# A node table of 98 places a lane instead of 105, and 109 rows of edges instead of 110, in a two-layer graph network

## The chip, the core and the metric

The kernel runs on one core of a Trainium2 chip. The metric is the device time of one execution in microseconds (us). All data are float32 or int32.

## What is computed

12,500 nodes with 256 features, 212,500 edges sorted by destination (12,500 of them are self edges). After a layer norm and a batch norm, two GIN layers follow: each sums the features of every node's neighbours, adds the node itself, and applies two dense layers with a batch norm between them.

```python
N, E, D = 12500, 212500, 256
h = relu(layernorm(x))
h = batchnorm(h, g0, b0)
for W1, b1, g, bt, W2, b2 in layers:          # two
    agg = segment_sum(h[src], dst, N)         # E rows of 256, sorted by dst
    h = relu(batchnorm((h + agg) @ W1 + b1, g, bt))
    h = relu(h @ W2 + b2)
out = x + relu(h)
```

## The kernel before

**Nodes.** Node n lies in lane n % 128 (the SBUF partition) and block n // 128; there are NB = 98 blocks. The sums and the features stand in `acc`, one column stretch of DP = 260 words (1040 bytes) for each block. For the gathers the features are also written to a table in HBM. In it a node has the place `lane * PITCH + block`, with PITCH = 105: 98 places with a node and 7 empty ones (zeros) in each lane, NPOS = 13,440 in all.

**Copies of the table.** Sources in one row of edges are sorted by place, and one gathered element may cover two edges whose places are 1, 2, 3, ... apart. For larger steps the table is stored four more times: the copy of stride s (3, 4, 5, 7) has places q, q + s, q + 2s, ... next to each other (`place_in`: residue q % s times NPOS / s, plus q // s). So NPOS must be a multiple of 3, 4, 5 and 7. A copy is written from `acc` with DMAs on SP's queue, generated by `strided_places`: for one stride it takes the lanes in `stride // gcd(stride, PITCH)` sets, and for each set and each residue of the blocks one DMA, of that many lanes by n blocks. `copies_of_blocks` does so for a group of GROUP = 14 blocks; GROUPS = 7 groups make the table. The empty places get zeros by `spare_places`, once for both tables, at L560.

**Edges.** The edges are cut into NR = 110 rows of LR = 1932 (the last is shorter), one row to a lane of the lists, sorted on VectorE within 2048 slots. The first RAWS = 14 rows are gathered edge by edge from the natural table in layer 0 while the sort still runs ("raw", 224 gathers of 128 rows at L679). For the others each row becomes T = 8 tiles of 128 elements; a tile is one indirect DMA on POOL (L697) of 128 elements with 4, 3, 3, 2, 2, 2, 2, 1 table rows each (`ROWS_OF`). Tiles 0 to 5 read the strided copies or the table, tiles 6 and 7 the natural table alone. PE multiplies each tile by one-hot matrices from VectorE (L830, 17 products a row) and VectorE adds the sums to `acc` (L1582).

**Order.** Layer 0: SP loads x and the edges, writes the empty places (L560), stores the table (L565), then issues the copies (L600), each behind a wait for the progress of the raw tiles (`raw_done`), so that they lie beside them. POOL's first strided gather waits for all copies (`copies_stored`, L711), and so does ACT's scaling of the sums (L1101). Then comes walk 0 over rows 14 to 109. After the batch norm the second product (`second_product`, `dense`) writes the new features block by block. SP stores them to the second table, chunk by chunk of 7 blocks (L565, last pieces L576); from the second chunk on it issues copies after each store, until 8 x 128 table rows are issued (`BESIDE`, L613); the rest follows after the last store (L617). POOL gathers tiles 6 and 7 of the first TWICE = 80 rows as soon as the natural table stands, and then waits for the copies of all groups (`group_stored`, L709) before the strided tiles of rows 0 to 79 and all tiles of the rest. ACT scales the sums of a group once its copies have landed (L1104).

If a check on the lists fails (a row that doesn't fit its tiles), `is_general` selects a slow general path on all engines.

Of the kernel before, what the change touches and what calls it, by code (L numbers as in the profile page):

```python
# [14 lines left out]
P = 128  # L15
# [7 lines left out]
NB = (N + P - 1) // P  # L23
# [7 lines left out]
DP = 260  # L31

PITCH = NB + 7
NPOS = P * PITCH
STRIDES = (3, 4, 5, 7)
TABLE = (1 + len(STRIDES)) * NPOS + 8

LR = 1932
NR = (E + LR - 1) // LR
TAIL = E - (NR - 1) * LR
SORT = 2048
# [37 lines left out]

UP = 512
PAD_SRC = 1000 * P + P - 1
SRC_CAP = 14000
REMOVED = float(2 ** 22)
DROPPED = float(2 ** 126)
WHOLE = 1.5 * 2 ** 23  # L90
# [7 lines left out]
RAWS = 14  # L98
# [6 lines left out]
RAW_HOTS = 3  # L105
LAST_EDGES = LR - (RAW - 1) * P
RAW_LISTS_AT = 8
# [5 lines left out]

NODES_PER_ROW = LR * N / E
NODE_TOL = 60
# [91 lines left out]

assert TWICE % 2 == 0 and NB % (2 * CH) == 0 and TAIL < LR and NR < P and RAW % AT_ONCE == 0
assert all(max(b for b in TILE_BEFORE[:k + 1] if b is not None) >= k - LANDINGS for k in range(LANDINGS, len(TILES)))
# [3 lines left out]
assert all(min(RAWS, PAIR_END[q] + 1) <= raws_merged_by(PAIR_ENDS[0][q]) for q in range(NPAIR))  # L213
assert all(2 * KC * P * (q % 2 + 1) <= raws_merged_by(PAIR_ENDS[0][q]) * DP for q in range(2))
assert PAIRS_BESIDE * RAW_GROUPS >= NPAIR and RAW % RAW_GROUP == 0 and 0 < LAST_EDGES <= P and 4 * SORT + RAW_INSIDE * DP <= RING * DP
assert SRC_CAP > NPOS + UP and all(NPOS % s == 0 and i + 1 == min(s, 6) - 2 for i, s in enumerate(STRIDES))
assert NB * (QUARTER + 1) <= RING * DP and 4 * SORT <= RING * DP and X_SLOTS * CH * D <= RING * DP

F32 = mybir.dt.float32
# [6 lines left out]
def build(nc, x, src, dst, g0, b0, W1a, b1a, g1, bt1, W1b, b1b, W2a, b2a, g2, bt2, W2b, b2b, out):  # L226
# [4 lines left out]
    with ctx:  # L231
        def sb(name, shape, dt=F32):
            return ctx.enter_context(nc.sbuf_tensor(name, shape, dt))
# [11 lines left out]
        src_rows = rows[:, GIVEN:2 * GIVEN]  # L245
        node_steps = rows[:, 2 * GIVEN:2 * GIVEN + LR]
        self_edges = rows[:, 3 * GIVEN:3 * GIVEN + LR]
# [30 lines left out]
        early = sb("early", [P, max(RAWS * DP, 4 * KC * P + 3 * KC * D + 2 * D)])  # L278
# [178 lines left out]
        def tile_rows(k, first, width):  # L457
            at_row = (TILE_AT[k] + first) * DP
            return rows[:, at_row:at_row + width]
# [17 lines left out]
            return bank[:, :].rearrange("p (j g) -> p j g", g=P)[:, :, 0:NR]  # L477

        def places(table, b0, b1):
            return table[0:NPOS, :].rearrange("(p b) f -> p b f", b=PITCH)[:, b0:b1, :]  # L480

        def block_rows(b0, b1, step=1):
            return acc[:, :].rearrange("p (b f) -> p b f", f=DP)[:, b0:b1:step, :]
# [1 line left out]
        def place_in(stride, q):  # L485

            return (1 + STRIDES.index(stride)) * NPOS + q % stride * (NPOS // stride) + q // stride

        def places_of(table, first_row, steps):
            return bass.AP(table.tensor, table.offset + first_row * DP, [[step * DP, n] for step, n in steps] + [[1, DP]])  # L490

        def strided_places(table, stride, b0, b1, of):

            lanes = stride // math.gcd(stride, PITCH)
            for lane in range(lanes):
                for first in range(b0, min(b0 + stride, b1)):
                    n = len(range(first, b1, stride))
                    yield (places_of(table, place_in(stride, lane * PITCH + first),
                                     [(lanes * PITCH // stride, P // lanes), (1, n)]),
                           of(first, n, stride)[lane:P:lanes])  # L500

        def copies_of_blocks(table, b0, b1):
            for stride in STRIDES:
                yield from strided_places(table, stride, b0, b1, lambda first, n, step: block_rows(first, first + (n - 1) * step + 1, step))

        zeros = early[:, 0:RAWS * DP].rearrange("p (b f) -> p b f", f=DP)

        def spare_places(table):
            yield places(table, NB, PITCH), zeros[:, 0:PITCH - NB]
            for stride in STRIDES:  # L510
                yield from strided_places(table, stride, NB, PITCH, lambda first, n, step: zeros[:, 0:n])
            yield table[TABLE - 8:TABLE, :], zeros[0:8, 0]

        EDGE_PIECES = ((0, 96), (96, NR - 1 - 96), (NR - 1, 1))
        EDGE_DMAS = 2 * len(EDGE_PIECES)
        CONST_DMAS = 1 + 8
        LATE_DMAS = 5
        SPARE = 16 * sum(1 for _ in spare_places(tables[0]))
        GROUP_COPIES = 16 * sum(1 for _ in copies_of_blocks(tables[0], 0, GROUP))
        COPIES = GROUPS * GROUP_COPIES  # L520
# [17 lines left out]
        def _(sp):  # L538
# [19 lines left out]
            for table in tables:  # L558
                for to, of in spare_places(table):
                    sp.dma_start(to, of).then_inc(spare_stored, 16)  # L560

            def store_rows(t, c, done, count):
                sp.wait_ge(done, count)
                b0, b1 = c * CH, (c + 1) * CH
                sp.dma_start(places(tables[t], b0, b1), block_rows(b0, b1)).then_inc(table_stored, 16)  # L565
# [6 lines left out]
            def store_last_rows():  # L572
                for at_block, end in LAST_PIECES:
                    b0, b1 = (NCH - 1) * CH + at_block, (NCH - 1) * CH + end
                    sp.wait_ge(y_out, b1)
                    sp.dma_start(places(tables[1], b0, b1), block_rows(b0, b1)).then_inc(table_stored, 16)  # L576
# [61 lines left out]
        def _(pool):  # L638
# [35 lines left out]
            for g in range(RAWS):  # L674
                for j in range(RAW):
                    k = g * RAW + j
                    if k >= RAW_SLOTS:
                        pool.wait_ge(raw_done, k - RAW_SLOTS + 1)
                    pool.indirect_dma_start(  # L679
                        raw_rows[k % RAW_SLOTS], None, tables[0][0:NPOS, :],  # L680
                        bass.IndirectOffsetOnAxis(raw_src[:, j * RAWS + g:j * RAWS + g + 1], 0)
# [6 lines left out]
            def gather(layer, g, t):  # L688
# [5 lines left out]
                if before is not None and before + 1 > freed:  # L694
                    freed = before + 1
                    pool.wait_ge(tiles_done, freed)
                pool.indirect_dma_start(  # L697
                    tile_rows(k, 0, ROWS_OF[t] * DP), None, tables[layer][0:NPOS if t >= LAST_STRIDED else TABLE, :],
                    bass.IndirectOffsetOnAxis(src_all[:, g * T + t:g * T + t + 1], 0)
# [426 lines left out]
        def _(dve):  # L1126
# [148 lines left out]
            def step(ins):  # L1275
                nonlocal sorted_to
                ins.then_inc(sort_step, 1)
                sorted_to += 1

            def after():  # L1280
                dve.wait_ge(sort_step, sorted_to)
# [76 lines left out]
            dve.wait_ge(steps_squared, 1)  # L1358
            step(dve.tensor_scalar(third_ints, keys, float(UP * P), float(SRC_CAP * P), ALU.add, ALU.min))
            after()  # L1360
# [44 lines left out]
            step(dve.tensor_scalar(key_ints, a, float(SINGLE), None, ALU.add))  # L1405
            step(dve.scalar_tensor_tensor(second, other_ints, float(SRC_CAP), second, ALU.is_ge, ALU.max))
            after()
# [393 lines left out]
```

## Time and profile before

| | |
|---|---|
| median of 3 runs | 2776.4 us (2771.52 to 2776.82) |
| profiled execution | 2784.43 us, its span 2782.6 us |
| PE matmul busy | 2371.1 us, 85% |
| PE weight load busy | 1827.6 us, 66% |
| POOL busy | 1815.2 us, 65% |
| DVE busy | 1739.1 us, 62% |
| ACT busy | 551.3 us, 20% |
| granted clock, mean | 0.94 |

The profile in 40 slices of 70 us; a digit is the busy share in tenths:

```profile
POOL 2058777777777777777740477677777777777720
PEclk8687766999999999999989899999999999999999
DMA  9387998888888888888848999888888888888868
GB/s 309 141 261 224 285 306 254 250 260 251 253 253 255 254 255 254 254 254 254 254 153 279 328 334 325 285 283 286 287 284 284 287 285 282 260 254 253 253 203 270
```

The first slices hold the loads, the layer norm and the store of the first table; slices 3 to 7 the raw tiles with the copies of layer 0; 7 to 20 walk 0; 21 to 22 the second product; 22 to 25 the copies of layer 1 with the natural gathers; 25 to 38 the strided gathers of walk 1. Engines: PE matmul, PEld its weight load, DVE VectorE, ACT ScalarE, POOL GpSimd, SP the engine whose queue issues the plain DMAs; SPq is time in which that queue is busy issuing.

### The profile page before, as it was taken

To read this page: it belongs to the slowest core of one execution; us is meant where nothing else is said; L and a number is where in the kernel's file an instruction comes from. 1 tells how busy PE (TensorE), PEld (TensorE's weight loads), DVE (VectorE), ACT (ScalarE), POOL (GpSimd) and SP (SyncE) were. 2 spreads that over 40 slices of the span, in tenths; PEclk is the share of its full clock that TensorE was granted. 3 is DMA by queue.
4 is the path that set the end of the run, shared out by engine and by line. 5 is a ranking of instruction groups with operands and counts; after the bars stand their busy time and mean duration, and the time that the engine had idled before them with its cause. 6 is when DMAs were issued, how large, how long until landed. Compare 5 with 4: busy or idle time off the path is not lost.

```text
span 2782.6 us, 30723 instructions
## 1 busy us (share of the span) xinstructions
PE 2371.1 (85%) x10215; PEld 1827.6 (66%) x10215; DVE 1739.1 (62%) x3502; ACT 551.3 (20%) x1605; POOL 1815.2 (65%) x1894
## 2 busy tenths in 40 slices
PE   1466777999999999999979566699999999988979
PEld 1134433878877777777758444588888888776767
DVE  7999997755555555555548577555555555544459
ACT  8975544300000000000009311000000000000038
POOL 2058777777777777777740477677777777777720
PEclk8687766999999999999989899999999999999999
DMA  9387998888888888888848999888888888888868
GB/s 309 141 261 224 285 306 254 250 260 251 253 253 255 254 255 254 254 254 254 254 153 279 328 334 325 285 283 286 287 284 284 287 285 282 260 254 253 253 203 270
DMA packets 309364, 734.28 MB, mean 264 GB/s; under 512 B 41510, under 2 KB 183730, under 8 KB 309198
## 3 DMA queue, kind: packets, MB, share of 16 engines
q0 software_dynamic: 149184, 550.97, 63.2%
q1 hardware_dynamic: 160014, 181.25, 20.8%
q8 instruction: 86, 1.41, 0.2%
q14 instruction: 80, 0.66, 0.1%
HBM read 579.47 MB, written 152.59 MB: 263 GB/s over the span
## 4 chain that ended last, share of the span: by engine, by line
PE 51%; DMA 23%; POOL 8%; SPq 8%; ACT 5%; issue 4%; DVE 1%; DVEq 0%; ACTq 0%; POOLq 0%
PE agg_ps L830 35%; DMA rows<-node_rows,src_all 17%; SPq L617 7%; PE sort_ps L955 6%; PE sort_ps L872 5%; POOL rows L697 5%; DMA rows<-node_rows,raw_list 4%; PE sort_ps L876 2%; DMA raw_more<-node_rows,raw_list 2%; PE agg_ps L779 2%; ACT acc L1001 2%; POOL raw_more L679 2%; ACT lane_code L988 1%; ACT lane_code L977 1%; POOL rows L679 1%
## 5 line engine op out<-in xcount | busy, mean ns | idle before, releaser
L697 POOL DMA_INDIRECT rows<-node_rows,src_all x1648 | 1558.2, 946 | 642.6 <-issue 346.4
L830 PE MATMUL agg_ps<-rows,work 128*128 128x256 f32 (+1 forms) x7004 | 1630.3, 387 | 188.9 <-DMA rows<-node_rows,src_all 140.8
L830 PEld LDWEIGHTS agg_ps<-rows,work 128*128 128x128 f32 x7004 | 1297.7, 191 | 494.3 <-issue 133.9
L1582 DVE SCALAR_TENSOR_TENSOR acc<-agg_ps,in_first,acc 128x256 f32 (+1 forms) x286 | 138.7, 485 | 944.1 <-PE agg_ps L830 856.7
L1032 ACT ACTIVATE bn_root<-bn_var 128x2 f32<-128x2 f32 x3 | 0.6, 203 | 1860.2 <-DVE bn_var L1168 1860.2
L679 POOL DMA_INDIRECT rows<-node_rows,raw_list x124 | 129.2, 1042 | 174.8 <-DMA node_rows<-acc 137.3
L1534 DVE TENSOR_TENSOR work<-lane_code,lane_ps 128x1024 f32<-128x1024 f32 (+1 forms) x206 | 228.1, 1107 | 1.0 <-issue 1.0
L955 PE MATMUL sort_ps<-early,work 128*128 128x256 f32 x784 | 175.3, 388 | 22.1 <-ACT work L1117 11.5
L955 PEld LDWEIGHTS sort_ps<-early,work 128*128 128x128 f32 x784 | 140.2, 194 | 57.5 <-issue 25.6
L1543 DVE TENSOR_TENSOR work<-lane_code,lane_ps 128x640 f32<-128x640 f32 x206 | 167.7, 814 | 0.0
L1117 ACT ACTIVATE work<-acc,bn_shift,bn_scale 128x128 f32<-128x128 f32 x392 | 166.5, 485 | 3.3 <-DVE bn_shift L1179 2.8
L779 PE MATMUL agg_ps<-rows,lane_code 128*128 128x257 f32 (+1 forms) x248 | 109.8, 562 | 59.6 <-DMA rows<-node_rows,raw_list 56.6
L1582 DVE SCALAR_TENSOR_TENSOR acc<-agg_ps,in_second,acc 128x256 f32 (+1 forms) x286 | 136.1, 476 | 0.0
L1524 DVE SCALAR_TENSOR_TENSOR work<-lane_ps,lane_code,work 128x128 f32<-128x128 f32 x412 | 130.5, 342 | 0.0
L679 POOL DMA_INDIRECT raw_more<-node_rows,raw_list x100 | 110.6, 1106 | 30.5 <-issue 23.5
L779 PEld LDWEIGHTS agg_ps<-rows,lane_code 128*128 128x128 f32 (+1 forms) x248 | 55.2, 260 | 106.6 <-DMA rows<-node_rows,raw_list 79.3
L1106 ACT ACTIVATE acc<-acc,self_scale 128x257 f32<-128x257 f32 (+1 forms) x196 | 79.0, 495 | 193.4 <-DMA node_rows<-acc 176.8
L1538 DVE TENSOR_TENSOR work<-lane_code,lane_ps 128x384 f32<-128x384 f32 x206 | 112.7, 547 | 0.0
L1345 DVE TENSOR_TENSOR work<-work,sort_ps 128x512 f32<-128x512 f32 x168 | 108.0, 684 | 2.9
L779 PE MATMUL agg_ps<-raw_more,lane_code 128*128 128x257 f32 x200 | 81.3, 530 | 32.2 <-DMA raw_more<-node_rows,raw_list 31.9
L872 PE MATMUL sort_ps<-early,w_a 128*128 128x256 f32 x392 | 107.2, 396 | 1.3 <-DVE early L1611 1.3
L1345 DVE TENSOR_TENSOR sort_ps<-work,sort_ps 128x512 f32<-128x512 f32 x168 | 108.2, 690 | 0.0
(246 smaller groups left out, 1844.8 us busy)
## 6 DMA issues: line engine op xcount, KB each, us to landing
node_rows<-acc SPq DMA_DIRECT2D x113, 260.0 KB, 6.3
rows<-node_rows,src_all POOLq DMA_INDIRECT x1648, 4.4
node_rows<-acc SPq DMA_DIRECT2D x27, 910.0 KB, 4.3
node_rows<-acc SPq DMA_DIRECT2D x57, 390.0 KB, 5.4
node_rows<-acc SPq DMA_DIRECT2D x28, 650.0 KB, 8.6
node_rows<-acc SPq DMA_DIRECT2D x114, 130.0 KB, 4.6
acc<-in_x SPq DMA_DIRECT2D x13, 896.0 KB, 11.0
rows<-in_x SPq DMA_DIRECT2D x13, 896.0 KB, 7.3
```

The lines of the kernel that those rows point to most:

```text
L617: sp.dma_start(to, of).then_inc(group_stored[i], 16)
L679: pool.indirect_dma_start(raw_rows[k % RAW_SLOTS], None, tables[0][0:NPOS, :], bass.IndirectOffsetOnAxis(raw_src[:, j * RAWS + g:j * RAWS ...
L697: pool.indirect_dma_start(tile_rows(k, 0, ROWS_OF[t] * DP), None, tables[layer][0:NPOS if t >= LAST_STRIDED else TABLE, :], bass.IndirectO ...
L779: pe.matmul(bank[:, 0:D + 1], raw_hots[n % RAW_HOTS][0:edges, (j - first) * P:(j - first + 1) * P], raw_rows[k % RAW_SLOTS][0:edges, 0:D + ...
L830: mm = pe.matmul(bank[:, 0:width], hot[:, unit * P:(unit + 1) * P], tile_rows(k, row, width), start=(start and n == 0), stop=(stop and n = ...
L872: mm = pe.matmul(to, w_a[layer][:, k, o * P:(o + 1) * P], sum_major[:, m % 2, k, :], start=(o == 0 and k == 0), stop=(last and k == KC - 1 ...
L955: mm = pe.matmul(mm_ps[b % 2][:, 0:D], act_major[:, b % CH, k, :], w_b[layer][:, k, :], start=(k == 0), stop=(k == KC - 1))
L1117: ins = act.activation(act_major[:, b % CH, k, :], half_block(b, k), ACT.Relu, bias=bn_shift[:, k:k + 1], scale=bn_scale[:, k:k + 1])
L1345: step(dve.tensor_tensor(place, low, high, op))
L1534: dve.tensor_tensor(hot[:, 0:2 * n * P].rearrange("p (j f) -> p j f", f=2 * P), codes[:, 0:n].unsqueeze(2).to_broadcast([P, n, 2 * P]), la ...
L1543: dve.tensor_tensor(hot[:, FIRST_AT[0] * P:(FIRST_AT[0] + m) * P].rearrange("p (j f) -> p j f", f=P), lanes[:, 0:m].unsqueeze(2).to_broadc ...
L1582: dve.scalar_tensor_tensor(to, sums, lanes[:, g:g + 1], to, ALU.mult, ALU.add).then_inc(sums_added, 1)
```

## The change

PITCH becomes 98, so that the 128 lanes fill the first 12,544 places (PLACES) without gaps. NPOS becomes 12,600, the next multiple of 3, 4, 5 and 7; the 56 spare places follow the whole table. A row of edges has 1950 instead of 1932, which makes 109 rows instead of 110. `strided_places` now counts the lanes of each set, since 128 isn't a multiple of the new numbers of sets. The spare places are written as one stretch for each copy and residue.

```diff
-PITCH = NB + 7
-NPOS = P * PITCH
+PITCH = NB
+PLACES = P * PITCH
+NPOS = 12600
...
-LR = 1932
+LR = 1950
...
-SRC_CAP = 14000
+SRC_CAP = 13500
...
-assert SRC_CAP > NPOS + UP and all(NPOS % s == 0 and i + 1 == min(s, 6) - 2 for i, s in enumerate(STRIDES))
+assert PAD_SRC // P + (P - 1) * PITCH + UP >= SRC_CAP > NPOS + UP and NPOS > PLACES and all(NPOS % s == 0 and i + 1 == min(s, 6) - 2 for i, s in enumerate(STRIDES))
...
-            return table[0:NPOS, :].rearrange("(p b) f -> p b f", b=PITCH)[:, b0:b1, :]
+            return table[0:PLACES, :].rearrange("(p b) f -> p b f", b=PITCH)[:, b0:b1, :]
...
-                                     [(lanes * PITCH // stride, P // lanes), (1, n)]),
+                                     [(lanes * PITCH // stride, len(range(lane, P, lanes))), (1, n)]),
                            of(first, n, stride)[lane:P:lanes])
...
-        zeros = early[:, 0:RAWS * DP].rearrange("p (b f) -> p b f", f=DP)
+        zeros = early[:, 0:DP]
 
         def spare_places(table):
-            yield places(table, NB, PITCH), zeros[:, 0:PITCH - NB]
+            yield table[PLACES:NPOS, :], zeros[0:NPOS - PLACES]
             for stride in STRIDES:
-                yield from strided_places(table, stride, NB, PITCH, lambda first, n, step: zeros[:, 0:n])
-            yield table[TABLE - 8:TABLE, :], zeros[0:8, 0]
+                for first in range(PLACES, PLACES + stride):
+                    n = len(range(first, NPOS, stride))
+                    yield table[place_in(stride, first):place_in(stride, first) + n, :], zeros[0:n]
+            yield table[TABLE - 8:TABLE, :], zeros[0:8]
```

## Rows read from the trace of the kernel before

**Rows 1.** The page: the span, and the chain that ended last.

```profile
span 2782.6 us, 30723 instructions
...
PE 51%; DMA 23%; POOL 8%; SPq 8%; ACT 5%; issue 4%; DVE 1%; DVEq 0%; ACTq 0%; POOLq 0%
```

**Rows 2.** POOL's timeline: start, duration, engine, line, tile, count, idle time before and its releaser.

```profile
469.07 0.94 POOL L697 DMA_INDIRECT rows<-node_rows,src_all  x1 [0.30 <-issue]
...
1430.84 0.95 POOL L697 DMA_INDIRECT rows<-node_rows,src_all  x1 [0.30 <-issue]
1558.84 0.94 POOL L697 DMA_INDIRECT rows<-node_rows,src_all  x1 [127.06 <-DMA node_rows<-acc]
...
1770.30 0.94 POOL L697 DMA_INDIRECT rows<-node_rows,src_all  x1 [11.69 <-DMA node_rows<-acc]
...
2668.69 0.94 POOL L697 DMA_INDIRECT rows<-node_rows,src_all  x1 [0.30 <-issue]
```

**Rows 3.** Busy time and instructions of each engine in stretches of 100 us.

```profile
core 0: us, PE busy (x) PEld busy (x) DVE busy (x) ACT busy (x) POOL busy (x), PEclk, DMA share, GB/s
700.00:800.00 100.00, 98.68 (x447) 79.48 (x446) 55.15 (x120) 0.00 (x0) 75.63 (x81) 1.00 0.82 254
2500.00:2600.00 100.00, 90.28 (x396) 71.10 (x396) 49.37 (x104) 0.00 (x0) 75.63 (x81) 1.00 0.82 254
```

**Rows 4.** Timeline of SP's queue, merged by line.

```profile
41.27 39.49 SPq L560 DMA_DIRECT2D node_rows<-early  x66
110.99 45.22 SPq L565 DMA_DIRECT2D node_rows<-acc  x14
...
161.85 290.53 SPq L600 DMA_DIRECT2D node_rows<-acc  x217
...
1475.80 1.53 SPq L613 DMA_DIRECT2D node_rows<-acc  x2
...
1552.39 210.42 SPq L617 DMA_DIRECT2D node_rows<-acc  x156
```

**Rows 5.** The chain of 1430 to 1790: shares by line, three pieces of it.

```profile
by line: SPq L617 56.1%; PE sort_ps L955 23.2%; issue 5.6%; PE agg_ps L830 5.5%; DMA node_rows<-acc 2.3%; PE sort_ps L872 1.5%; DMA rows<-node_rows,src_all 1.3%; SPq L613 1.2%; PE sort_ps L876 1.0%; SPq L576 0.9%; POOL rows L697 0.3%; DVE e
...
1597.29 6.87 SPq L617
...
1695.26 0.61 SPq L617
...
1761.12 8.32 DMA node_rows<-acc
```

**Rows 6.** DMA view of 1475 to 1770: packets, and each queue's share of 16 engines.

```profile
q1 hardware_dynamic: 55952, 64.31, 70.9%
q0 software_dynamic: 10240, 31.96, 32.7%
```

**Rows 7.** DMA view of 9 to 16.9, of 2779.8 to 2781.15, of 2781.2 to 2782.6.

```profile
DMA packets 840, 1.88 MB, mean 238 GB/s; under 512 B 60, under 2 KB 679, under 8 KB 840
...
GB/s 303 364 364 364 334 303 455 273 334 364 394 303 303 455 303 273 394 394 273 304 274 91 183 182 304 364 303 334 394 394 303 303 425 243 182 61 61 0 0 0
DMA packets 403, 0.38 MB, mean 282 GB/s; under 512 B 32, under 2 KB 403, under 8 KB 403
...
q1 hardware_dynamic: 403, 0.38, 82.8%
...
DMA packets 98, 0.09 MB, mean 61 GB/s; under 512 B 14, under 2 KB 98, under 8 KB 98
```

**Rows 8.** DMA issues of the whole span: KB each, us from issue to landing.

```profile
node_rows<-acc SPq DMA_DIRECT2D x113, 260.0 KB, 6.3
...
work<-in_dst SPq DMA_DIRECT2D x1, 98.2 KB
...
out<-acc SPq DMA_DIRECT2D x1, 84.0 KB
```

**Rows 9.** DMA view of 170 to 450: the gathers' queue.

```profile
q0 software_dynamic: 9813, 27.22, 36.2%
```

## The prediction

> **What bounds the kernel now.** I read the page's chain first. It names PE for half the span, which makes the walks look like matrix work, but a chain follows only the last releaser; POOL and SP stand in it too [rows 1]. So I read POOL's timeline. In both walks a gather starts every 1.25 us, whatever PE does: 768 strided gathers of layer 0 from 469.07 to 1430.84, 160 natural ones of layer 1 from 1558.84 on, which end 11.69 us before 1770.30, and 720 strided ones from there to 2668.69: (1430.84 - 469.07) / 767 and (2668.69 - 1770.30) / 719 are both 1.25 [rows 2]. The stretches of 100 us say the same: 81 gathers and 75.63 us of POOL in each, PE busy 99% in one and 90% in the other [rows 3]. The walks run at POOL's issue rate.
>
> Between the walks stands a second bound. A strided gather reads one of four strided copies of the table, and the first one waits until all copies have landed. SP issues them: 217 DMAs from 161.85 in layer 0, and in layer 1 61 between the table stores from 1475.80 on and 156 more until 1761 [rows 4]. In layer 1 the last copy lands at 1761.12 + 8.32 = 1769.4 and the gather follows at 1770.30; the chain of that stretch gives SP's L617 56.1% [rows 5]. In layer 0 it doesn't bind: the last copy is issued at 452.4, and the gather at 469.07 follows its predecessor after the usual 0.30 us [rows 2, 4]. What the copies cost is DMA time: from 1475 to 1770 the 16 engines are busy 70.9 + 32.7 = 103.6% [rows 6].
>
> **The change, part by part.**
>
> *One row of edges less.* 109 rows instead of 110: each walk loses a full row of 8 tiles at 1.25 us, 10 us. The last 8 strided gathers of each walk are what falls away, and the walks are POOL's from their first gather to their last, so **-20 us** counts in full. 1950 columns instead of 1932 in some setup operations on VectorE, and 30 edges instead of 12 in the last raw tile of a row, cost nothing I can measure: those are below 1% of operations that are not the longest there.
>
> *Spare places.* 66 stores of zeros become 42 smaller ones. They run from 41.27 to 80.8, and SP then waits for ACT's rows until 111 [rows 4]: 30 us of cover. If that were gone, 24 issues of 0.6 us would be worth 14 us. I take 0.
>
> *The copies.* With a pitch of 98 the lanes fall apart into classes: a stride s needs s/gcd(s, pitch) sets of lanes, each with its own DMAs. Before, that was 1, 4, 1, 1 sets for strides 3, 4, 5, 7; now it is 3, 2, 5, 1. For 14 blocks that makes 9 + 8 + 25 + 7 = 49 DMAs instead of 3 + 16 + 5 + 7 = 31; 343 a layer instead of 217. The 7168 rows of 1040 bytes for each group of 14 blocks stay. What changes is how many lanes a DMA has: 128 and 32 before; now 43, 43, 42 for stride 3; 64 for stride 4; 26, 26, 26, 25, 25 for stride 5; 128 for stride 7.
>
> Which engines such a DMA uses is the question. The DMA view counts a packet for each row and, below 512 bytes, one for each engine that ends its share. Around 2780 us two stores of 128-row blocks end with 32 such packets, 16 each. The last store has 84 rows (84 KB): 98 packets, 84 rows and **14** endings, so 14 engines with 6 rows each, not 16. The six loads of edges have 96, 13 and 1 rows, each twice; they end with 60 = 2 x (16 + 13 + 1) packets [rows 7, 8]. Two readings fit all four sizes. *Equal shares*: the engines used are the largest number up to 16 that divides the rows. *Rounded shares*: each engine takes ceil(rows/16), and the last may take fewer. They part at 43: equal shares give **1** engine (43 is prime), rounded shares 15. The 84 rows exclude a third reading, rows dealt out one by one, which would have used 16 engines. Between the other two the trace doesn't decide. I take equal shares, since every DMA in it has the same number of rows on each engine that it uses, and no row shows an engine with an odd rest.
>
> The Trainium skill ("DMA: Bandwidth & Descriptors", section "Why a DMA increments its semaphore by 16 and not by 1") states equal shares, too: the largest count up to 16 that divides the slowest dimension of both sides, and on the queues of SP always the lowest-numbered engines. By it 43 lanes run on one engine, and it speaks against this change; by rounded shares the sum would be the 2774 us below. The trace agrees at 84, 13 and 1; no run here shows 43.
>
> Load of the busiest engine for each group, in rows of 1040 bytes: stride 3: two sets of 43 lanes x 14 blocks on one engine, 1204, and 42/14 x 14 = 42; stride 4: 2 x 4 x 14 = 112; stride 5: 3 x 2 x 14 = 84 on 13 engines and 2 x 5 x 14 = 140 on 5; stride 7: 8 x 14 = 112. If the shares always begin at the same engine, it carries 1694 rows against 448 before; in 7 groups 11,858 against 3136. If each DMA began elsewhere, the order in SP's queue would still put up to six 43-lane DMAs behind each other, but they could overlap; that is the low side.
>
> Price of a row on one engine: two looks. Near the end 0.38 MB take 82.8% of 16 x 1.35 us, so 21.2 GB/s of a busy engine, 49 ns for 1040 bytes; from 1475 to 1770, with all engines full, 64.31 MB take 70.9% of 16 x 295 us, 19.2 GB/s, 54 ns. The best slices show 364 GB/s, 45.7 ns [rows 6, 7]. With 15 engines nearly idle the first is nearer: 49 ns x 11,858 = **581 us** a layer.
>
> *Layer 0.* The copies begin at 161.85. The same engine carries a sixteenth of the 224 raw gathers, 8 rows each: 1.86 MB at 20.7 GB/s (rate of the gather queue: 31.96 MB in 32.7% of 16 x 295 us [rows 6]), 90 us. End of the copies 161.85 + 581 + 90 = 833. The raw tiles and VectorE's sort still end near 468 beside it. The first strided gather moves from 469 to 833: **+364 us**; all behind it moves along. Behind the copies in SP's queue stand the weight loads (L602 on), which wait for a point inside the walk anyway; ACT's scaling of the sums waits for the copies too (L1101), as it did, and takes 6 us for the blocks that the first row needs.
>
> *Layer 1.* From 1475.80 (all times as if nothing had moved before): copies 581, the 12 chunks of table stores still to come (910 KB each, a sixteenth, 21.2 GB/s) 33, natural gathers 31.96 MB / 16 at 20.7 GB/s, 97. End 2187 against 1769.4: **+417 us**. The second product's 80 us, the 160 natural gathers (200 us at 1.25) and the wait for table stores queued behind 43-lane copies (SP gets to the last of them after about 3300 rows on that engine, 160 us) all end before: 1475.8 + 160 + 33 + 200 = 1869. ACT's scaling of the sums waits group by group for the same copies (L1104), VectorE's adds wait for ACT, and so the natural visits up to row 79, which reach block 73, wait for the sixth of seven groups; that lands a seventh of the time, 100 us, before the last. After the copies the walk goes at 1.25 us a gather again.
>
> Sum against the profiled execution, 2784.4 us (span 2782.6 [rows 1]): + 364 + 417 - 20 = 3545. The median of the runs lies 8 us lower: **3537 us**.
>
> **Rivals.**
>
> *Rounded shares.* 43 lanes on 15 engines at 3 rows. The busiest engine carries 42 x 3 + 112 + 140 + 112 = 490 rows a group, 42 more than before, 294 in a layer, 14 us at 49 ns. In layer 0 the copies end near 459 (452.4 and 6.3 us to landing [rows 8]), so 14 us later is 4 us of wait; in layer 1 all 14 count. 2784.4 + 4 + 14 - 20 - 8 = **2774**: not slower. It decides if a 43-row DMA ends on more than about ten engines. For it: the trace has no prime above 16. Against it: see above. Small shifts make it a little faster or the same.
>
> *SP's issue as the bound.* If the rows are spread, 126 more issues a layer remain, at 0.61 us each [rows 5], 77 us, if SP can't queue ahead. Layer 1 alone exposes it: 2784.4 + 77 - 20 - 8 = **2833**. Against it: 343 x 0.61 = 209 us is less than the 294 us that the data takes in layer 1, and SP's issues there stretch to 6.87 us when the engines are full, so it does queue ahead.
>
> *A cheaper or dearer engine.* At 45.7 ns a row (gathers at that rate too) layer 0 is +317 and layer 1 +367: 3440. At 54 ns and raw gathers at 16.8 GB/s (27.22 MB in 36.2% of 16 x 280 us [rows 9]) it is +444 and +487: 3687. Same mechanism, other size. A lone queue that can't keep its engine full would go further; nothing here prices that, so the top gets 100 us more.
>
> *It doesn't do what it says.* 1950 edges in 2048 slots leave denser rows; should one row not fit its tiles, the kernel takes its general path, with loops of 98 steps for every four columns, many times slower. Nothing in the profile speaks for it; 0.02.
>
> **How the numbers follow.** Equal shares on one engine 0.87, rounded shares 0.08, SP's issue 0.03, general path 0.02. The range holds eight in ten within the first case: from 3440, less 50 for overlap between DMAs, to 3687 plus 100: **3390 to 3787**. It leaves out the two middle cases and the general path. A measurement of this kernel tells about 0.2% apart, 6 us. Faster by that takes rounded shares with less than their full price, 0.04; within it 0.05; slower 0.91.
>
> **What would show it.** POOL's wait for the copies near 833 us instead of none, and again some 417 us longer in layer 1; DMA share of slices falling to one or two tenths with GB/s under 50 while 43-lane copies run; SP's issues of L600 and L617 taking many us each in groups of six; gathers 8 fewer in each walk, still at 1.25 us. The prediction is wrong if the DMA share stays at nine tenths during the copies; then it is the rounded case. It is off in size if the slices show another rate for the one engine than 21 GB/s.

## The result, and the profile after

The changed kernel takes 3574.53 us (median of 4 runs, 3571.87 to 3575.25), the one before 2775.11 us (4 runs, 2771.52 to 2776.82). The ratio is 1.288, 95% interval 1.286 to 1.2901: slower by 799 us, as forecast. 3537 us was predicted, 1% less than measured and inside the range. Of all runs told here one, of e8, was far from the others of its kernel (3991.24 us, at a mean granted clock of 0.567 instead of 0.94); the ratios leave it out.

The page of the changed kernel: span, POOL's busy tenths, DMA share and rate in 40 slices of 89 us, and the engines' shares of the chain.

```profile
span 3572.6 us, 30769 instructions
...
POOL 1187720003777777777710074310177777777750
...
DMA  5455532226888888888824466432488888888877
GB/s 169 171 150 160 155 111 83 84 83 189 264 251 253 254 254 252 253 253 253 253 81 144 145 183 178 143 109 84 144 284 284 285 284 284 284 273 253 253 227 246
...
PE 38%; SPq 28%; DMA 16%; POOL 9%; issue 5%; ACT 4%; DVE 0%; DVEq 0%; POOLq 0%; ACTq 0%
```

The PE share of the chain fell from 51 to 38%, SP's queue rose from 8 to 28% [rows 1]. Slices 7 to 9 and 22 to 28 (from 1) are new. In 7 to 9 POOL stands still and the rate is 83 or 84 GB/s; 22 to 28 hold the copies of layer 1, with the natural gathers in 24 to 27, and end at 84 GB/s. The walks between and behind have the rates of before. The mean granted clock was 0.837 instead of 0.94, but the table below shows the walks no longer than before, so the clock is not what costs the time.

POOL's timeline gives the stages (start, duration, line, idle time before and its releaser): the last raw gather, the first strided gather of layer 0, its last, the first strided gather of layer 1, its last.

```profile
470.30 0.94 POOL L682 DMA_INDIRECT rows<-node_rows,raw_list  x1 [0.30 <-issue]
...
850.25 0.94 POOL L700 DMA_INDIRECT rows<-node_rows,src_all  x1 [379.00 <-DMA node_rows<-acc]
...
1802.01 0.95 POOL L700 DMA_INDIRECT rows<-node_rows,src_all  x1 [0.30 <-issue]
...
2567.62 0.94 POOL L700 DMA_INDIRECT rows<-node_rows,src_all  x1 [167.19 <-DMA node_rows<-acc]
...
3456.88 0.95 POOL L700 DMA_INDIRECT rows<-node_rows,src_all  x1 [0.30 <-issue]
```

SP's queue, merged by line, shows what POOL waited for: the stores of zeros and of the first table, the copies of layer 0 (L603), the first of layer 1 (L616) and the rest (L620).

```profile
41.52 16.42 SPq L563 DMA_DIRECT2D node_rows<-early  x42
...
111.21 45.20 SPq L568 DMA_DIRECT2D node_rows<-acc  x14
...
162.35 682.91 SPq L603 DMA_DIRECT2D node_rows<-acc  x343
...
1846.29 39.07 SPq L616 DMA_DIRECT2D node_rows<-acc  x5
...
2047.27 515.39 SPq L620 DMA_DIRECT2D node_rows<-acc  x249
```

Against [rows 2, 4]:

| stage | before | after | difference |
|---|---|---|---|
| first strided gather of layer 0 | 469.07 | 850.25 | +381.2 |
| walk 0, first to last gather | 961.8 | 951.8 | -10.0 |
| last gather of walk 0 to the first copy of layer 1 | 45.0 | 44.3 | -0.7 |
| first copy of layer 1 to the first strided gather | 294.5 | 721.3 | +426.8 |
| walk 1, first to last strided gather | 898.4 | 889.3 | -9.1 |
| rest | 113.9 | 115.7 | +1.8 |
| span | 2782.6 | 3572.6 | +790.0 |

The table adds up. Two waits for copies are +808 us, and the row less gives 19 us back. The mechanism can be looked at directly. An *ending* is, as in the prediction, one of the packets below 512 bytes, which each engine leaves when its share of a DMA ends. The DMA view of 580 to 617, where the moving data is of 43-lane copies alone and POOL is idle:

```profile
GB/s 11 24 22 21 20 21 21 21 20 21 21 20 21 21 21 20 21 21 20 21 21 21 20 21 21 20 21 21 20 21 21 21 20 21 21 20 21 21 21 20
DMA packets 746, 0.77 MB, mean 21 GB/s; under 512 B 3, under 2 KB 746, under 8 KB 746
...
q1 hardware_dynamic: 746, 0.77, 6.7%
```

21 GB/s through the whole stretch, and 6.7% of 16 engines, which is 107% of a single one. Of the 746 packets only 3 are endings: three 43-lane DMAs end here, one ending each. The chain of 520 to 620 shows SP held up by them (start, duration): a copy of 43 lanes and 5 blocks is 215 rows, and the next issue waits 10.58 us for it, 49.2 ns a row; with 4 blocks 8.69 us. A copy of 26 lanes (stride 5) takes SP 0.81 us.

```profile
by line: SPq L603 109.1%; issue 2.2%
...
524.38 10.58 SPq L603
...
535.01 8.69 SPq L603
...
552.04 0.81 SPq L603
```

Do copies of one queue simply run one after another, each on whatever engine? The end of a run of 43-lane copies tells. Three windows of the DMA view, 530.5 to 540.8, 541 to 544, and 541.1 to 548.5:

```profile
DMA packets 208, 0.22 MB, mean 21 GB/s; under 512 B 0, under 2 KB 208, under 8 KB 208
...
DMA packets 61, 0.06 MB, mean 21 GB/s; under 512 B 0, under 2 KB 61, under 8 KB 61
...
GB/s 22 22 17 22 22 17 22 22 22 17 22 22 22 17 22 22 22 112 264 225 253 253 113 236 191 230 264 219 231 253 253 315 337 354 343 337 360 332 337 343
DMA packets 1220, 1.21 MB, mean 163 GB/s; under 512 B 61, under 2 KB 1220, under 8 KB 1220
```

A copy of 5 blocks ends between the first two windows; the last one of this run (43 lanes, 4 blocks, 172 rows) follows it and at 49 ns a row needs until about 549.5. Yet from 544.3 on the copies issued behind it (42 lanes, from 543.74) move on the other engines, and 61 endings come before it can have ended. So copies don't wait for each other as such. What waits is a row on an engine that is still busy with earlier ones, and 43-lane copies that follow each other do wait: they are on the same engine.

The count of endings of the whole run is the sharpest reading. The page's line of packets:

```profile
DMA packets 303335, 720.47 MB, mean 202 GB/s; under 512 B 41132, under 2 KB 181096, under 8 KB 303170
```

By equal shares the packets below 512 bytes must be: 1856 gathers x 16 = 29,696; 2048 elements of 4 bytes in 8 loads of vectors; the endings of the 98 loads and stores that aren't copies or zeros, 1524; zeros 402; and for each group of 14 blocks 6 x 1 + 3 x 14 + 8 x 16 + 15 x 13 + 10 x 5 + 7 x 16 = 533, times 14 groups, 7462. The sum is 41,132, which is the page's number to the packet. With 43 lanes on 15 engines it would be 1176 more from that stride alone.

### The profile page after: what moved, and what is told of

It is laid out like the page before. It is cut to its first block, busy times and chain, and to the rows that moved or that the text cites. A ratio compares the mean times of both kernels' runs of the same rounds, so it can differ in the third digit from the quotient of the medians.

```text
span 3572.6 us, 30769 instructions
## 1 busy us (share of the span) xinstructions
PE 2382.7 (67%) x10147; PEld 1818.0 (51%) x10147; DVE 1730.5 (48%) x3486; ACT 552.7 (15%) x1605; POOL 1803.9 (50%) x1878
## 2 busy tenths in 40 slices
DMA packets 303335, 720.47 MB, mean 202 GB/s; under 512 B 41132, under 2 KB 181096, under 8 KB 303170
## 4 chain that ended last, share of the span: by engine, by line
PE 38%; SPq 28%; DMA 16%; POOL 9%; issue 5%; ACT 4%; DVE 0%; DVEq 0%; POOLq 0%; ACTq 0%
PE agg_ps L833 25%; SPq L620 14%; DMA rows<-node_rows,src_all 12%; SPq L603 10%; POOL rows L700 6%; PE sort_ps L958 5%; PE sort_ps L875 4%; SPq L616 3%; DMA rows<-node_rows,raw_list 2%; PE sort_ps L879 2%; POOL rows L682 1%; POOL raw_more L682 1%; DMA raw_more<-node_rows,raw_list 1%; ACT acc L1004 1%; PE agg_ps L782 1%
## 5 line engine op out<-in xcount | busy, mean ns | idle before, releaser
L782 PE MATMUL agg_ps<-raw_more,lane_code 128*128 128x257 f32 x200 | 92.7, 567 | 35.9 <-DMA raw_more<-node_rows,raw_list 34.8
```

Source lines behind the costliest of these rows:

```text
L782: pe.matmul(bank[:, 0:D + 1], raw_hots[n % RAW_HOTS][0:edges, (j - first) * P:(j - first + 1) * P], raw_rows[k % RAW_SLOTS][0:edges, 0:D + ...
```

## The experiments

The experiments are called by the first part of their labels (e5 and so on) and told in the order of the argument. Each is compared with runs of the kernel before that were made beside it; their medians were 2777.26 us (e3 to e6), 2773.37 (e1, e7 to e9), 2774.13 (e10) and 2778.21 (e12 to e14).

**Only the number of lanes (e5, e6).** The kernel before keeps its pitch of 105 and its 110 rows; only the stride-3 copies are cut, into neighbouring lanes.

```diff
-                    yield (places_of(table, place_in(stride, lane * PITCH + first),
-                                     [(lanes * PITCH // stride, P // lanes), (1, n)]),
-                           of(first, n, stride)[lane:P:lanes])
+                    at = 0
+                    for m in (43, 43, 42) if stride == 3 else (P // lanes,):
+                        l0 = lane + at * lanes
+                        yield (places_of(table, place_in(stride, l0 * PITCH + first),
+                                         [(lanes * PITCH // stride, m), (1, n)]),
+                               of(first, n, stride)[l0:l0 + (m - 1) * lanes + 1:lanes])
+                        at += m
```

> The kernel before (pitch 105, 110 rows), with one edit: each stride-3 copy of 128 neighbouring lanes is cut into 43, 43 and 42 neighbouring lanes. Same bytes, same places, 42 more DMAs a layer, no lane is skipped. Equal shares from the same first engine: two sets of 43 lanes x 14 blocks on one engine, so 1204 + 42 + 3 x 112 = 1582 rows a group on it, 11,074 a layer; at 50 ns a row, with the gathers' share, the copies of layer 0 end near 805 us (+336) and those of layer 1 take 683 instead of 294 us (+389): 3501 us. Rounded shares: 2776 to 2790 us. If what is slow were lanes with a step of 3 or 5 (the pattern in SBUF) or the change's new places in HBM, this kernel stays at 2776 us. If each additional DMA cost what it seems to in the changed kernel, (3574 - 2775 + 20) / 252 = 3.2 us: 84 more are 2776 + 273 = 3050 us.

Measured: 3462.27 us (one run), 39 us below the forecast. Rates of the DMA view from 700 to 780, and the end of POOL's wait in layer 0:

```profile
GB/s 321 266 26 21 21 21 21 21 21 21 122 21 21 21 21 21 21 21 21 21 21 122 21 21 21 21 21 21 21 24 218 183 177 192 196 244 342 341 313 306
...
784.58 0.94 POOL L701 DMA_INDIRECT rows<-node_rows,src_all  x1 [313.45 <-DMA node_rows<-acc]
```

The same 21 GB/s, in a kernel whose table, places, rows and lane steps are those of before. The wait in layer 0 is 313 us (the first strided gather at 784.58, forecast 805), and layer 1 takes 653.7 us (forecast 683), 47.8 ns for each of 13,666 rows; the rows were priced a little too high. The cut alone costs 685 us, so a loss of this size needs neither the step of the lanes nor the new places nor the denser rows. The packets of its page:

```profile
DMA packets 309364, 734.28 MB, mean 212 GB/s; under 512 B 41510, under 2 KB 183730, under 8 KB 309198
```

This is the line of the kernel before, number for number: 43, 43 and 42 lanes leave 1 + 1 + 14 endings, 128 lanes left 16.

> The same cut of the kernel before with other sizes: 48, 48 and 32 neighbouring lanes for stride 3. As many DMAs as with 43, 43 and 42, and the same bytes, but each size is a multiple of 16. Equal shares: 3 + 3 + 2 = 8 rows an engine and block, as with 128 lanes, so 2776 us, within 0.3%. A cost of each additional DMA: 3050 us by the price of 3.2 us, or by the 0.61 us of an issue 2776 + 26 = 2802 us at most.

The edit is the same with (48, 48, 32). Measured: 2786.23 us, ratio 1.0032 (1.0019 to 1.0044). As many DMAs as with 43, 43, 42, the same bytes, and 676 us less. It is 9 us above the kernel before, a little more than expected; more on that below.

```profile
DMA packets 310900, 734.29 MB, mean 264 GB/s; under 512 B 43046, under 2 KB 185266, under 8 KB 310734
```

43,046 against 41,510 endings: 1536 more. That is 3 residues x 14 groups = 42 triples of DMAs, and 6 more in the stores of zeros, 48, of 16 + 16 + 16 against 1 + 1 + 14 = 16 endings: 48 x 32 = 1536, exact.

**Numbers that divide, but badly (e14).** The same edit with (65, 63).

> The kernel before with stride 3 cut into 65 and 63 neighbouring lanes; neither is prime. Equal shares: 65 on 13 engines with 5 rows, 63 on 9 with 7, so 12 rows a block on the first engine instead of 8; 56 rows a group, 392 a layer, at 50 ns +20 us in layer 1 and up to +5 in layer 0: 2800 us. Rounded shares: 5 + 4 = 9 rows, +5 us: 2780 us. If every count that isn't a multiple of 16 went on one engine, 128 rows a block: above 3500 us.

Measured: 2799.44 us, ratio 1.008 (1.0065 to 1.0096); its page:

```profile
DMA packets 309652, 734.29 MB, mean 262 GB/s; under 512 B 41798, under 2 KB 184018, under 8 KB 309486
```

Equal shares give 13 + 9 endings for each pair of these DMAs and a total of 41,798 (rounded shares: 13 + 16, 42,134). The count is exact again, so equal shares hold for counts that aren't prime. The time agrees with the forecast, but less well than it looks: by POOL's timeline layer 1 took 303.7 us and layer 0 began 3 us later, +9 and +3 against before, where +20 and +5 were expected; the rest lies in the offset that is told below. On the fullest engine are 3528 rows of copies, 672 of stores and 1920 of gathers in layer 1: 303.7 us / 6120 = 49.6 ns, against 294.5 / 5728 = 51.4 before. With all engines equally full the row came out a little dearer.

**Mending the change, one count at a time (e3, e4).** In the changed kernel the same loop takes its pieces from a table; lanes that are neighbours within a set of step `lanes` stay so.

```diff
+                    for m in {43: [42, 1]}.get(len(range(lane, P, lanes)), [len(range(lane, P, lanes))]):
```

> The changed kernel, where each copy DMA of 43 lanes is split into 42 lanes and 1 lane; the 25- and 26-lane DMAs stay. 42 DMAs more a layer (385). Equal shares: 42 lanes go on 14 engines, 3 rows each, the single lane adds one; the first engine carries 2 x 14 x 4 + 42 + 112 + 224 + 112 = 602 rows a group instead of 1694. With gathers and stores 6918 rows in layer 1, 345 us at 50 ns against 294 before: +50; layer 0 ends near 465 to 470: 0 to +5; the row less -20: 2776 + 50 + 3 - 20 = 2809 us, 765 us faster than the changed kernel by adding DMAs. If the step of the lanes or the number of DMAs were the cause: 3574 us or more.

Measured: 2858.29 us (one run). 716 us of the loss go with 84 *more* DMAs in the two layers, so the number of DMAs was not their cause. The kernel is 49 us slower than expected: the strided gathers begin at 498 instead of 469 in layer 0, and layer 1 takes 362 us. This run doesn't say why; e4 and e7 point at the issues. Its page counts 42,616 endings, 1484 more than the change. The expectation, one ending for the single lane, would give 1176; with 5 + 5 + 4 endings for its copies of 5, 5 and 4 blocks it is 1484, exact. When only one lane is left, the blocks are the outermost dimension above one, and they are what is shared out.

```diff
+                    for m in {43: [32, 11], 25: [16, 9]}.get(len(range(lane, P, lanes)), [len(range(lane, P, lanes))]):
```

> The changed kernel with every bad count split: 43 lanes into 32 + 11, 25 into 16 + 9; 26 and 42 stay (13 and 14 engines). 65 DMAs a group, 455 a layer against 343 and 217. Equal shares: 3 x 42 + 112 + 140 + 112 = 490 rows a group on the fullest engine, as in the rounded case: layer 1 has 6134 rows, 307 us, +12; layer 0 hidden; 2776 + 12 - 20 = 2768 us. Issue as the bound: 455 x 0.61 = 278 us of issues in layer 1 beside 307 us of data; if they don't overlap fully, up to 60 us more, 2830 us. If the number of DMAs were the cause of the 800 us: above 4000 us.

Measured: 2923.76 us, ratio 1.0527 (1.0509 to 1.0544). Better shares, and slower by 65 us than e3. SP's queue in layer 0; from the chain two neighbouring issues of 32 and 11 lanes (stride 3) and two of 16 and 9 (stride 5); and the rates from 470 to 530:

```profile
162.33 367.16 SPq L607 DMA_DIRECT2D node_rows<-acc  x455
...
486.92 0.60 SPq L607
...
487.56 0.81 SPq L607
...
513.55 0.60 SPq L607
...
514.20 0.76 SPq L607
...
GB/s 135 64 52 52 49 343 328 277 275 265 157 149 149 119 170 242 347 317 268 216 194 137 69 106 90 94 82 90 60 58 57 42 46 52 52 52 41 200 345 297
```

455 issues in 367.16 us are 0.81 us each, waits included. The first pair moves 160 and 55 rows, 224 KB, and the rate there is about 149 GB/s; the second moves 16 x 3 rows, 50 KB, in 0.60 us and 9 x 3 rows, 28 KB, in 0.76 us, and the rate is 41 to 60 GB/s. In both stretches the rate is what the issues bring, so here the issue is the bound. An issue took 0.60 us with 16 or 32 lanes, 0.76 with 9, and 0.79 to 0.81 with 11, 26 or 42; in the changed kernel one of 25 lanes, on 5 engines, took 0.70 to 0.72. My expectation compared sums (278 us of issues, 307 us of data); it should have compared them stretch by stretch, since the rate follows the issues within a few us.

**Fewer, larger copies (e7, e8).** On e4, and for e8 on the kernel before. The first list is layer 1's, the second layer 0's.

```diff
-GROUPS = NB // GROUP
+BOUNDS = (0, 14, 42, 70, 98)
+GROUPS = len(BOUNDS) - 1
...
+        BOUNDS_0 = (0, 98)
...
-                    for to, of in copies_of_blocks(tables[1], i * GROUP, (i + 1) * GROUP):
+                    for to, of in copies_of_blocks(tables[1], BOUNDS[i], BOUNDS[i + 1]):
```

> The changed kernel with 43 lanes split into 32 + 11 and 25 into 16 + 9 as in e4, and with fewer, larger copies: layer 0 copies the whole table as one group of 98 blocks (65 DMAs instead of 455), layer 1 in four groups of 14, 28, 28 and 28 blocks (260 instead of 455). The share of the fullest engine is the same as in e4 (35 rows a block); only the number of issues falls. If e4 lost its 150 us because SP couldn't issue fast enough (its traces show 0.60 us for 16 or 32 lanes and 0.77 to 0.80 for 9, 11, 26 or 42), this one hides the issues: 260 x 0.7 = 182 us beside 307 us of data in layer 1, so 2776 + 12 - 20 = 2768 us, at most 2800 where the small stride-5 copies still starve the engines. If e4 lost them to the uneven shares or to small packets on some engines, it stays near 2924 us.

Measured: 2809.88 us, ratio 1.0132 (1.0116 to 1.0149). SP's queue in layer 0 and after the second product, and the end of POOL's wait in layer 1:

```profile
162.10 303.17 SPq L609 DMA_DIRECT2D node_rows<-acc  x65
...
1577.33 218.90 SPq L626 DMA_DIRECT2D node_rows<-acc  x172
...
1803.74 0.94 POOL L706 DMA_INDIRECT rows<-node_rows,src_all  x1 [21.59 <-DMA node_rows<-acc]
```

114 us better than e4 with the same shares, so most of e4's loss was the issues. It is still 10 us above the top of what was expected (2768 to 2800): layer 0 ends 13 us late, of which the single group of 98 blocks accounts for 8 (e8), and layer 1 takes 327 us instead of 294.5, of which the fuller engine was to cost 12. A further variant, with groups of 28, 28, 21 and 21 blocks in both layers (e11), has no result: in it `acc` could be overwritten before a copy had read it. So what is left of e7's loss isn't taken apart.

> The kernel before (pitch 105, 110 rows) with the groups of e7: 31 copies for the whole table in layer 0, 124 in layer 1. Its copies are limited by the engines' data in layer 1 (103.6% busy) and hidden in layer 0, so fewer issues are worth nothing: 2776 us, within 0.3%. If the groups themselves were worth something, it shows here and has to be taken off e7.

Measured: 2786.2 us (median of four runs, 2784.45 to 2787.25), ratio 1.0046 (1.003 to 1.0062), just outside what was expected: layer 0 begins its walk 8 us later, layer 1 takes 285.5 us, 9 less. The groups by themselves gain nothing.

**The parts alone (e9, e1).** e7 and the changed kernel with 110 rows.

```diff
-LR = 1950
+LR = 1932
```

> e7 with 1932 edges a row, so 110 rows: the pitch of 98 alone, without the row that it saves. Eight gathers more in each walk at 1.25 us: e7 + 20 us. If the walks weren't POOL's, less.

Measured: 2833.74 us, ratio 1.0215 (1.0197 to 1.0232), 23.9 us above e7.

> The changed kernel with 1932 edges a row, so 110 rows: the pitch alone, copies as in the change. Copies unchanged, eight gathers more in each walk: 3574 + 20 = 3594 us. If the denser rows had a part in the slowdown, it would be faster than 3574 instead.

Measured: 3598.27 us (one run), 23.7 us above the changed kernel. Its copies of layer 1 take 721.0 us, as in the change; its wait in layer 0 ends at 856.9, 6.6 us later, and its two walks are 18 us longer. So the pitch carries the whole loss. The row is worth some 24 us by the medians and 18 by the walks; whether the 6.6 us belong to it, one run can't tell.

**Another way to write the copies (e10, e12, e13).** Strides 3 and 5 from the finished table in HBM, one DMA for each residue; strides 4 and 7 as before.

```diff
+        FLAT = (3, 5)
+
+        def flat_copies(table):
+            for stride in FLAT:
+                n = NPOS // stride
+                for first in range(stride):
+                    at = place_in(stride, first)
+                    yield table[at:at + n, :], places_of(table, first, [(stride, n)])
...
+            sp.wait_ge(table_stored, TABLE_DMAS[1])
+            for to, of in flat_copies(tables[1]):
+                sp.dma_start(to, of).then_inc(flat_stored, 16)
```

> The changed kernel, where the copies of strides 3 and 5, the ones whose lane sets divide badly, are no longer written from acc: each residue is one DMA from the finished table in HBM to the copy in HBM (8 DMAs a layer, 4200 or 2520 rows, which by equal shares run on 15 engines, 280 or 168 rows each). Strides 4 and 7 stay (15 DMAs a group of 14 blocks, all multiples of 16). The fullest engine then carries 16 x 98 + 1680 = 3248 rows a layer of copies against 3136 before and 11,858 in the change; SP issues 113 DMAs. If a row from HBM to HBM takes an engine the same 50 ns as one from acc, layer 1 needs +6 us and layer 0 is hidden: 2776 + 6 - 20 = 2762 us, under the kernel before. If reading the rows from HBM costs more (26 MB more are read beside 64 written and 32 gathered in the same 295 us), layer 1 grows; at the 327 GB/s that this stretch showed before, by 80 us: 2836 us.

Measured: 2773.49 us, ratio 1.0 (0.9991 to 1.001) to the kernel before. 11 us slower than the 2762 forecast, but the whole 799 us are back, with 113 issues a layer (105 from acc, 8 from HBM). Rates from 1700 to 1740 and from 1745 to 1769; the queues and the new copies from 1480 to 1790; the end of POOL's wait:

```profile
GB/s 334 384 338 267 309 319 295 296 234 290 359 352 370 395 353 278 317 344 336 322 358 333 335 266 292 208 227 277 363 310 276 255 370 376 377 334 377 352 355 355
...
GB/s 250 298 329 350 329 309 272 314 313 298 276 213 196 258 291 229 227 262 246 205 224 199 213 277 265 328 272 296 336 222 104 104 83 62 49 38 21 9 0 0
...
q1 hardware_dynamic: 51563, 59.60, 60.5%
q0 software_dynamic: 11617, 37.51, 37.7%
...
q14 instruction: 11, 0.09, 0.1%
...
node_rows<-node_rows SPq DMA_DIRECT2D x3, 4265.6 KB, 65.0
node_rows<-node_rows SPq DMA_DIRECT2D x5, 2559.4 KB, 39.9
...
1768.88 0.94 POOL L723 DMA_INDIRECT rows<-node_rows,src_all  x1 [24.79 <-DMA node_rows<-node_rows]
```

Layer 0 is hidden (first strided gather at 469.52) and layer 1 takes 302.9 us, 8 more than before. The 4 MB copies need 65 us from issue to landing, and while they are alone, after the last natural gather, the rate is about 200 to 330 GB/s and then falls off over the last 6 us. A second version (e12) sets them between the other copies, a third (e13) also cuts them at a multiple of 16.

> e10 with the HBM-to-HBM copies of layer 1 set between the remaining copies from acc, instead of behind them. In e10 the last 26 us before the strided gathers hold almost only those copies, and the rate falls from 322 to 214 GB/s. If that is because a copy from HBM to HBM alone can't keep its engines full, mixing them removes most of it: 8 to 10 us, 2764 us. If the engines' packets are the bound all the way, nothing changes: 2773 us.

Measured: 2779.74 us, ratio 1.0006 (0.9997 to 1.0015); layer 1 takes 303.4 us. The order made no difference; the expected 8 to 10 us aren't there.

> e12 with each HBM-to-HBM copy cut at a multiple of 16 rows (4192 + 8, 2512 + 8), 8 more DMAs a layer. Equal shares: 16 engines instead of 15, 1575 + 8 rows on the fullest one instead of 1680: 97 rows at 50 ns, 5 us in layer 1, so e12 - 5 us.

Measured: 2781.98 us, ratio 1.0016 (1.0007 to 1.0025); layer 1 takes 301.6 us. 16 engines instead of 15 (its page counts 144 endings more than e10's, which is what 15 to 16 and 8 new endings give for 16 copies) buy 2 us at best and the median doesn't show them. No version beats the kernel before.

## Why the prediction was right

*The mechanism* held at each point that was named. POOL waits for copies that it never waited for in layer 0, and longer in layer 1. Equal shares, which the trace of before couldn't tell from rounded ones, are shown by the endings of the change, e5, e6 and e14 to the packet and by e5 against e6 in time. The same count comes out exact for e3 (with the blocks shared out for the single lane), e4 (46,116), e7 (38,115) and e10 (37,136), too. That the shares of all DMAs begin at the same engine, on which the whole sum rests, is seen for 43-lane copies that follow each other, and that the queue doesn't just run one copy after another is seen at 544.3. For the other counts it is shown only indirectly: if their shares began elsewhere, the load of 11,858 + 672 + 1920 = 14,450 rows wouldn't sit on one engine, and layer 1 wouldn't take 721.3 us, 49.9 ns for each of these rows.

Two statements of the prediction didn't come out, without harm to the sum. No slice fell under 50 GB/s: of the slices of 89 us that hold copies the lowest reads 83, since each holds other copies, too, and the 21 GB/s show only in short windows. And the 160 natural gathers of layer 1 took 349 us (2051.4 to 2400.4) instead of 200; eight rows of each lie on the full engine. They still ended 167 us before POOL could go on.

*The sum.* Price of a row: 49 ns taken, 49.2 measured on a lone DMA, 49.9 in layer 1, 688 us / 13,650 rows = 50.4 in layer 0, where the raw gathers go on the same engine. Layer 0: +364 forecast, +381 measured; layer 1: +417 against +427. The mis-sized term of layer 0 is probably the raw gathers' share, 90 us at 20.7 GB/s. At the 16.8 GB/s of [rows 9], which I had put only in the upper case, it is 111 us, and the copies would end near 854, against 850.25 measured for the gather behind them. The changed kernel's own view of 170 to 460 gives 16.4 GB/s (27.64 MB in 36.4% of 16 x 290 us):

```profile
q0 software_dynamic: 9971, 27.64, 36.4%
```

A price of 50.4 ns for every row would fit as well; the trace doesn't part the two. Of layer 1's 10 us some 5 are the landing of the last copy (SP's last issue ends at 2562.7, the gather starts at 2567.62), which the sum left out; the rest is within the rounding of the row's price (1 ns of it is 14 us). The low bound of the range took 364 GB/s as the best slices, though [rows 7] show up to 455; those slices are 34 ns long and hold some 15 packets, so neither is a rate to price by, and the measured time doesn't come near that bound. The row less: -20 forecast, -19 in the timelines, -24 in the medians of e9 and e1. The spare places: 0, and SP's stores of zeros end at 57.9, long before 111.21.

*The rest of the miss.* I took 8 us off, because the profiled execution of before (2784.4) lay above its median. The changed kernel has no such offset: profiled 3574.66, median 3574.53. 8 of the 37 us come from there. The same offset runs through the experiments. None of the 55 other executions of the kernel before reached 2784.43 (the highest took 2783.18). e6 and e8 have the stages of before within a few us in their profiles, yet their medians are 9 to 13 us above the median of before; e10's profile is 12 us under that of before, and its median is equal. Which stages were longer in that one profiled execution can't be seen, since the others have no profile; that stays open, and differences of 10 us to the kernel before aren't explained here.

*The rivals.* Rounded shares fell with the counts. SP's issue as the bound was not what slowed the change, but I dismissed it too easily: with the shares mended layer 1 takes 97 us more than before (12 of them expected from the shares) and layer 0 66 (e4). My price for it, 0.61 us, was that of a DMA on 16 engines; those on fewer cost 0.70 to 0.81. The case of rounded shares was given 2774 us. e4 has that load on its fullest engine and needs 2924, but it also has 455 issues a layer instead of 343, so the 2774 us stay untested. The general path wasn't taken.

The Trainium skill ("DMA: Bandwidth & Descriptors", section "Why a DMA increments its semaphore by 16 and not by 1") states this rule of the largest divisor; the runs agree at 84, 65, 63, 43, 42, 26 and 25 rows. The same section says that for k < 16 engines the issuing sequencer writes the missing 16 - k itself. The runs agree with a cost of that kind: 0.60 us with 16 or 32 lanes, 0.76 to 0.81 with 9, 11, 26 or 42, 0.70 to 0.72 with 25. The cost doesn't grow with the number missing (25 lanes use the fewest engines, 5). That it is this write which takes the 0.1 to 0.2 us is not shown.

## What to carry to other kernels

Count the outermost dimension of every DMA that a change of layout produces (here the lanes), and take its largest divisor up to 16: that many engines worked in every kernel here. A prime such as 43 puts 224 KB on one of them, at 21 GB/s instead of over 300, and SP's queue is held up behind it. If the counts can't be made multiples of 16, splitting them trades the imbalance for issues of 0.6 to 0.8 us, which pays only while each DMA carries more data than the engines move in that time; a copy with another outermost dimension may be better than either.

A gain of one row in 110 can be right to the microsecond and still be the smallest part of a change. Look for what the new number does to the shapes of transfers that aren't on the critical path yet.

## What the runs showed that I had not expected

A row on the fullest engine costs nearly the same beside 15 idle engines (49.2 ns) as beside 15 full ones (51.4 ns in layer 1 before). I had taken 49 and 54 ns for the two, further apart than they are. So one engine moves 20 to 21 GB/s here in copies of such rows, whatever the others do, and a stretch is as long as its fullest engine, as long as the issues keep up (in e3, e4 and e7 they don't seem to).

An HBM-to-HBM copy of rows of 1040 bytes costs an engine about as much as one from SBUF: layer 1 of e10 with 3248 + 672 + 1920 = 5840 rows on the fullest engine took 302.9 us, 51.9 ns a row, though it reads 26 MB more from HBM in the same time.
